# Routed pairs of blocks before the last batch's routing, and two shared tiles at the end (transformer layer with a mixture of experts, one core)

## The reference

```python
x = x + attn(layernorm(x), Wq, Wk, Wv)            # (8, 512, 256), one head
y = layernorm(x)
shared = (silu(y @ sg.T) * (y @ su.T)) @ sd.T     # inner width 512
probs = sigmoid(y @ router.T + bias)
scores, idx = top_k(probs, 2); scores /= scores.sum(-1)
w[t, idx] += scores
routed = einsum(silu(y @ gate_w[e]) * (y @ up_w[e]), down_w[e], w)
x = x + shared + routed
```

## Time and profile before

| | us |
|---|---|
| median of 3 runs | 563.93 |
| lowest and highest run | 558.07, 567.77 |
| span of the profiled execution | 555.3 |
| PE busy in it | 518.0 (93%) |
| DVE, ACT, POOL busy | 369.8, 301.0, 288.9 |
| mean granted PE clock | 0.986 of full |

### The profile page before, as it was taken

One profiled execution on the slowest core, in us unless ns is written; L12 is line 12 of the kernel. 1 busy time (PEld: TensorE's weight loads), 2 busy tenths in 40 slices (PEclk: granted clock), 3 DMA queues, 4 the chain that ended last, 5 costly groups with the idle time before them and its releaser, 6 DMA issues.

```text
span 555.3 us, 14903 instructions
## 1 busy us (share of the span) xinstructions
PE 518.0 (93%) x4757; PEld 425.5 (77%) x4757; DVE 369.8 (67%) x980; ACT 301.0 (54%) x580; POOL 288.9 (52%) x242
## 2 busy tenths in 40 slices
PE   4889988999999999997999999999999999999992
PEld 3557766788878888886767788888787888888881
DVE  5788998689887878899747555445454454454551
ACT  3989877678777676744233443433343433434341
POOL 4466677668676765857022344452444434434443
PEclk9999999899999999998899999999999999999998
DMA  8799848949694947414465965764846536345443
GB/s 271 201 181 208 178 127 158 217 133 209 161 208 141 194 127 170 155 70 136 131 115 85 98 107 69 103 83 60 108 59 89 73 60 97 55 65 78 62 58 38
DMA packets 139351, 68.55 MB, mean 123 GB/s; under 512 B 114608, under 2 KB 132336, under 8 KB 139280
## 3 DMA queue, kind: packets, MB, share of 16 engines
q1 hardware_dynamic: 126128, 48.84, 43.5%
q0 software_dynamic: 13152, 18.76, 19.4%
HBM read 19.46 MB, written 23.08 MB: 77 GB/s over the span
## 4 chain that ended last, share of the span: by engine, by line
PE 65%; DVE 12%; DMA 8%; SPq 5%; ACT 5%; issue 3%; POOL 1%; POOLq 0%; ACTq 0%; DVEq 0%
PE bank L2216 29%; PE bank L2240 15%; PE bank L2547 4%; PE bank L2322 3%; PE bank L2564 3%; DMA v<-xnrow 2%; PE bank L2625 2%; PE bank L2347 2%; PE bank L2392 2%; DMA xn2t<-xrow 2%; PE bank L2369 2%; PE bank L2640 2%; SPq L405 2%; DMA x<-x 1%; DVE h L1470 1%
## 5 line engine op out<-in xcount | busy, mean ns | idle before, releaser
L2216 PE MATMUL bank<-xn2t,w 128*128 128x256 f16 x1608 | 184.9, 273 | 1.3 <-DVE th L1653 1.1
L2216 PEld LDWEIGHTS bank<-xn2t,w 128*128 (+1 forms) x1608 | 155.2, 98 | 24.3 <-DVE th L1653 2.2
L1644 DVE SCALAR_TENSOR_TENSOR th<-th,bank 128x512 f32<-128x512 f32 x83 | 56.6, 682 | 55.2 <-ACT th L989 54.1
L2240 PE MATMUL bank<-w,h 128*128 (+1 forms) x768 | 91.5, 273 | 0.0
L943 ACT ACTIVATE h<-th 128x512 f16<-128x512 f32 (+1 forms) x69 | 42.9, 622 | 84.6 <-DVE th L1653 78.3
L989 ACT ACTIVATE th<-bank 128x512 f32<-128x512 f32 x83 | 49.2, 593 | 62.1 <-PE bank L2216 47.6
L2240 PEld LDWEIGHTS bank<-w,h 128*128 128x128 f16 x768 | 74.0, 98 | 10.4 <-DVE x L1676 0.3
L866 POOL DMA_INDIRECT out<-p,wm x28 | 43.9, 1569 | 67.2 <-ACT p L1323 27.3
L1470 DVE TENSOR_TENSOR h<-th,h 128x512 f16<-128x512 f32 (+1 forms) x69 | 50.6, 733 | 38.3 <-ACT h L943 38.1
L734 POOL TENSOR_TENSOR w<-wst,w 128x768 f16<-128x768 f32 x36 | 59.1, 1645 | 18.9 <-ACT w L943 18.7
L758 POOL DMA_INDIRECT rows<-xrow,sidx x56 | 56.5, 1009 | 17.0 <-issue 13.3
(11 more groups left out here) (188 smaller groups left out, 808.4 us busy)
## 6 DMA issues: line engine op xcount, KB each, us to landing
wst<-w_all SPq DMA_DIRECT2D x36, 384.0 KB
x<-x SPq DMA_DIRECT2D x8, 512.0 KB, 5.6
out<-x SPq DMA_DIRECT2D x8, 512.0 KB, 4.0
rows<-xrow POOLq DMA_DIRECT2D x1, 1192.5 KB, 6.6
rows<-xrow,sidx POOLq DMA_INDIRECT x56
out<-p,wm POOLq DMA_INDIRECT x28
xn2t<-rows SPq DMA_TRANSPOSE x26
wm<-rows SPq DMA_DIRECT2D x26, 9.0 KB, 2.4
```

The costliest lines, as they stand in the source:

```text
L1644: d.scalar_tensor_tensor(out=tb, in0=tb, scalar=1.0, in1=G[half][:, :], op0=ALU.add, op1=ALU.mult).then_inc(f_sg, 1)
L2216: ins = mm(dst, w_ap(j, ws, m * MAT + k * I + (2 * half + i) * P, P), moving(ms * KD + k), start=(cnt == 0), stop=(cnt == 3 * KD - 1))
L2240: ins = mm(o[:, a * D:(a + 1) * D], hb[:, (hs * KI + i) * TT + a * P:(hs * KI + i) * TT + (a + 1) * P], w_ap(j, ws, 2 * MAT + i * D, D), s ...
```

## The change

1. The size of the table of 512-row blocks is set by what six batches surely fill: `QUADS` is 5 instead of 9. Their table is made from the counts after batch 5 (`counts_seen`), while batch 7's attention ends. Blocks are now laid from the beginning of each expert's rows, and the zeros stand behind the last row; they are copied there when the final counts are known (`zero_ends`), so the zeros at the start are one block of 128 rows.
2. PE starts the routed phase after shared tile 12, with three groups that are pairs only (`plain_groups`, pairs 0 to 5). Shared tile 13's down, batch 7's transposes, logits and final counts, and on DVE its routing and the other three tables (pairs, singles, halves, in one chain of 56 steps) are threaded into these groups.
3. Pairs 6 to 25 follow with singles and halves as before, in groups up to 12 (before: up to 11 and a last group with finer pieces). The fifth 512-row block, pairs 24 and 25, is the last. Pairs 8 to 23 are single pairs.
4. `out_base` of batch 7 writes `x1` with attention only. Shared tiles 14 and 15 come at the very end, their inputs being still in SBUF. When all adds have landed, SP reads their rows back from `out` to `x1`, DVE adds the two downs there, and SP writes them with plain DMAs.
5. The weights' last pieces are scaled earlier on ACT, directly one after the other, and made on POOL between the scatters of batch 6.

```diff
-QUADS = (TOPK * T // HP - 7 * E) // 8
+SEEN = 6
+QUADS = -(-(SEEN * S * TOPK - E * (2 * TT - 1)) // (2 * TT))
+EARLY = 2 * (QUADS - 1)
+LATE = 2
+AHEAD = SHARED - LATE
+PLAIN = 3
@@ SP
+            load_pair_rows(pair0, 0, 2 * AHEAD - 2)
+            load_pair_rows(pair1, 1, 2 * AHEAD)
+            load_pair_aux(pair0, 0, 0, 0)
+            load_pair_aux(pair1, 1, 0, 0)
+            out_base(5)
+            out_base(7)
+            out_base(6)
+            for n in (2, 3, 4):
+                pair_rows(n)
+                pair_aux(n)
+            pair_rows(5)
+            zero_ends(0, E // 2)
+            pair_rows(6)
+            zero_ends(E // 2, E)
+            pair_aux(5)
             sp.wait_ge(tab2, T2_STEPS)
+            rows_complete()
...
             sp.wait_ge(y_out, ALL_ADDS)
+            for i in range(LATE):
+                sp.dma_start(tile_of(AHEAD + i), tile_rows(AHEAD + i)).then_inc(back_in[i], 16)
+            sp.wait_ge(y_read, AHEAD + PAIRS + 1)
+            sp.dma_start(tile_rows(AHEAD), tile_of(AHEAD)).then_inc(out_done, 16)
@@ POOL
             w_low(30)
             scatter(5, 5, 8)
             last_identity()
+            w_low(31)
+            w_low(32)
+            scatter(6, 0, 1)
+            w_low(33)
+            scatter(6, 1, 2)
+            w_low(34)
+            scatter(6, 2, 3)
+            w_low(35)
+            scatter(6, 3, 5)
             rstd2(7)
             put_idx(7)
+            scatter(6, 5, 8)
...
+            y_add(0)
+            scatter(7, 0, 4)
+            y_add(1)
+            scatter(7, 4, 8)
+            for n in range(2, 2 * PLAIN):
+                y_add(n)
@@ ACT
             split_h(11, 1)
+            w_scale(32)
+            w_high(32)
             tanh(12, 0)
+            w_scale(33)
+            w_high(33)
             tanh(12, 1)
             split_h(12, 0)
+            w_scale(34)
+            w_high(34)
+            tanh(13, 0)
+            split_h(12, 1)
+            w_scale(35)
+            w_high(35)
@@ DVE
             places(6)
+            ffn_gate(12, 0)
+            ffn_up(12, 0)
+            ffn_gate(12, 1)
+            ffn_up(12, 1)
+            add_shared(10)
+            row_numbers(6)
+            table_of_quads()
+            ffn_low(12, 0)
+            ffn_gate(13, 0)
+            ffn_low(12, 1)
+            add_shared(11)
...
+            def plain_groups():
...
+                ffn_low(t + 1, 1)
+                route(7)
+                ffn(t + 2, 0)
+                weights(7)
+                places(7)
+                row_numbers(7)
+                ffn(t + 2, 1)
+                ffn(t + 3, 0)
+                k = table_of_pairs()
+                ffn(t + 3, 1)
+                k = table_of_singles(k)
+                ffn(t + 4, 0)
+                table_of_halves(k)
+                ffn(t + 4, 1)
@@ PE
             shared_gate_up(13, 0)
-            last_transposes(0)
-            last_transposes(1)
+            shared_down(11, 0, 2)
             shared_gate_up(13, 1)
+            shared_down(12, 0, 2)
...
+            def plain_groups():
+                pair_gate_up(0, 0)
+                shared_down(13, 0, 2)
+                expert(1)
+                pair_gate_up(0, 1)
+                last_transposes(0)
+                last_transposes(1)
+                pair_gate_up(1, 0)
+                expert(2)
+                pair_down(0)
+                pair_gate_up(1, 1)
+                logits(7)
+                pair_gate_up(2, 0)
...
+            def last_group():
+                t = AHEAD + PAIRS
+                gate_up(t, 0, 0, half_batch(xn24(B - 1), 0), True)
+                pair_down(PAIRS - 1)
+                gate_up(t, 1, 0, half_batch(xn24(B - 1), 0), True)
+                gate_up(t + 1, 0, 0, half_batch(xn24(B - 1), 1), True)
+                gate_up(t + 1, 1, 0, half_batch(xn24(B - 1), 1), True)
+                down(t, 0)
+                last_down()
```

More of the change, by code:

```diff
@@ new lines, in zero_ends, with rows_complete @@
+            def zero_ends(first, last):
+                sp.wait_ge(tab2, 2)
+                for e in range(first, last):
+                    end = sp.value_load(end_tab[0:1, e:e + 1], min_val=0, max_val=ROWS - P)
+                    sp.dma_start(rows[ds(end, P), :], rows[SPARE:SPARE + P, :]).then_inc(pads_in, 16)
+            def rows_complete():
+                sp.wait_ge(rows_in[0], scattered(B - 2))
+                sp.wait_ge(rows_in[1], scattered(B - 1))
+                sp.wait_ge(pads_in, 16 * E)
@@ L650, in _ @@
+            for a in range(2):
+                n = 2 * (SHARED - 1) + a
+                sp.wait_ge(z_put, a + 1)
+                sp.dma_start(out[n * P:(n + 1) * P, :], x1[:, n * D:(n + 1) * D]).then_inc(out_done, 16)
+            sp.wait_ge(out_done, 16 * (B + 3))
         @block.gpsimd
@@ L1454, in _ @@
+                if s - FIRST_HALF < HALVES:
+                    half_h(s - FIRST_HALF)
+                ffn_half_and(t + 1, 1, *[PAIRS + SINGLES + s - FIRST_HALF] * (s - FIRST_HALF < HALVES))
+            def last_group():
+                t = AHEAD + PAIRS
+                ffn_half_and(t, 0, PAIRS - 1)
+                y_copy_of(PAIRS - 1)
+                ffn_half(t, 1)
+                ffn_half(t + 1, 0)
+                ffn_half(t + 1, 1)
+            plain_groups()
             first_groups()
-            for i in range(2, GROUPS - 1):
+            for i in range(PLAIN + 2, GROUPS):
@@ L2174, in _ @@
+            plain_groups()
+            first_groups()
+            with dve.Fori(PLAIN + 2, SINGLES - 4 + PLAIN) as i:
                 group(i)
-            group(SINGLES - 4, single=False)
-            for i in range(SINGLES - 3, GROUPS - 1):
+            group(SINGLES - 4 + PLAIN, single=False)
+            for i in range(SINGLES - 3 + PLAIN, GROUPS):
                 group(i, single=False, half=False)
-            ffn(SHARED + PAIRS - 2, 0)
-            ffn(SHARED + PAIRS - 2, 1)
-            ffn(SHARED + PAIRS - 1, 0)
@@ L2679, in group, with last_down @@
                 gate_up(t + 1, 1, expert(2 * i + 1), pair_moving(1), False, covered=True, mats=(1,))
-            def down_parts(t, j, pieces):
-                pe.wait_ge(y_read, t)
-                for low, chunks, parts in pieces:
-                    pe.wait_ge(f_lo, t * 2 + low)
-                    for a in parts:
-                        for i in chunks:
+            def last_down():
+                t = AHEAD + PAIRS + 1
+                pe.wait_ge(fs_h, SINGLES)
+                pe.wait_ge(fh_h, HALVES)
+                pe.wait_ge(ys_read, SINGLES)
+                pe.wait_ge(yh_read, HALVES)
+                for half in range(2):
+                    pe.wait_ge(f_lo, t * 2 + half + 1)
+                    for a in range(2):
+                        for i in (2 * half, 2 * half + 1):
```

761 lines of the change are left out of this document (351 added, 410 removed).

## The result

| | before | after |
|---|---|---|
| median, us | 561.97 (14 runs) | 568.14 (14 runs) |
| lowest and highest | 558.07, 567.77 | 564.78, 576.47 |
| span of the profiled execution | 555.3 | 567.5 |

The ratio is 1.0125, 95% interval 1.0092 to 1.0157: the change makes the kernel slower by some 6 us. The forecast was 561.0, a little faster; the time lies in its range, on the other side of no change.

The account below looks back on a forecast made before the run. TensorE, busy 93% of the span, was taken as the bound. Added 4.0 + 4.2 + 7.5 = 15.7 us against 18.6 removed: 2.9 us less, moving the 563.93 us median to 561.0, range 552 to 571.

Parts of the forecast that it names:

- What is removed: Waits around the old transition 5.3, slow clock 2.5, last tile's wait 0.5, old tail 10.3: together 18.6 us gained.
- One, the approach to pair 0: From shared tile 12 to pair 0, TensorE waits add 4.0 us; bounds 1.0 and 5.6, 2.5 more if the clock falls.
- The holds: Before pair 0, VectorE and GpSimd hold each other during five low parts of weights: 0.5 us added.
- The clock: TensorE's 1.2 GHz level after idling before pair 0: 2.5 us more, only on top of the upper bound.
- term two: Batch 7's routing and tables under three plain groups: TensorE waits add 4.2 us, bounds 1 and 6.
- two or three of 1 to 3 us: Sign of the forecast: that many TensorE waits on low parts of h between 275 and 300 us.
- Three, the end: Tail after TensorE's last matmul, with adds landing, read-back and last additions: 7.5 us, bounds 6.3 and 10.
- Rival D: Chain of adds becomes the bound, falls 5 us behind TensorE, and the readback follows: 566 us; chance 0.12.
- Rival C: Idle TensorE and its slow clock move instead of going, through piece 33's load and VectorE's holds: 570.4 us; chance 0.12.
- pair 0 near 242: Sign of the forecast: pair 0, the first routed work after the shared tiles, starts near 242 us.
- no clock below 1.00: Sign of the forecast: TensorE's clock stays at full level between 240 and 300 us.
- a wait above 3 us before pair 0: Sign that the forecast is wrong: TensorE shows such a wait on the approach to pair 0.

Follow-up runs that it names:

- e_nohold: Changed kernel with GpSimd writing zeros by memset instead of the low parts of weight pieces 31 to 35: ratio 0.9958 to the kernel before.
- e_low_order: Changed kernel with only GpSimd's queue reordered, low part of piece 33 ahead of batch 6's first scatter, 34 and 35 later: ratio 1.0030 to the kernel before.
- e_places: Changed kernel with VectorE making the places of batch 6 ahead of the low part of tile 11's second half: ratio 1.0027 to the kernel before.
- after_timed_b: The changed kernel unedited, timed as a control on the fifth chip: ratio 1.0058 to the kernel before.
- after_again: The changed kernel unedited, run once for a second profile: 560.45 us.
- after_timed: The changed kernel unedited, timed as a control on the second chip: ratio 1.0081 to the kernel before.
- e_front: Changed kernel with VectorE's, GpSimd's and ScalarE's queues reordered before pair 0, batch 7's tables left as they were: ratio 0.9936 to the kernel before.

## Why the prediction was wrong

**What is removed** was right. The second profile of before has it too: 3.1 us of wait on the add, the slow clock behind it, and 10.1 us from the last matmul to the end, all of which the changed kernel no longer has in that form.

**One, the approach to pair 0, is the step that failed**: "I add 0.5: 3.5 + 0.5 = 4.0 us". It measured 10.0 us here, 9.5 to 10.5 in three more profiles of the same kernel, beyond the upper bound of 5.6, and with the clock's 2.5 beyond 8.1. Its walk was sound in one part: tanh of tile 12's second half came 9.4 us after tile 12's start (236.11 and 226.70), for 8.8. Three things in it were not:
- *The holds.* 0.5 us were set for them, in spite of five low parts and rows that showed 4.12 and 1.49. They fell on the table, 2.27 + 2.36, where the walk took 3.0 for it and it took 7.2, and on the low part and the cast around `places(6)`, 1.4 and 1.3: 7.0 us in all beyond the usual lengths. `e_nohold` puts all of them, with the clock that follows the waits, at 6.2 us of distance (21.3 against 27.5, some 0.4 of it perhaps from GpSimd's shorter work), `e_low_order` those in the table at 2.1. The rule of the Trainium skill (SBUF — State Buffer, "SBUF: two separate sides"), which the prediction kept out of its sum, would have given a loss; by that rule and by these rows the held operation ends with the GpSimd instruction (0.02 and 0.04 us behind it).
- *A queue that was not walked.* PE's second half of tile 12 needs `pos` from `places(6)`, which stood behind a low part of tile 11 on VectorE: 2.1 us. Of these 1.4 are the hold of that low part (2.05 us for 0.69), and without it 0.8 is left (`e_nohold`). Taken alone the order costs nothing (`e_places`), since the next wait is longer.
- *The clock.* After both waits TensorE ran at 1.2 GHz for most of a piece, 1.7 + 1.4 = 3.1 us. The text had 2.5 for that, outside the sum, for a wait over 3 us. One of 2.13 us was enough here, and one of 2.00 in `after_timed_b`; in `after_again` and `after_timed` the clock stayed up behind 2.14 and 2.13, and fell behind the longer wait alone.

With the order put right and all else as changed (`e_front`) the kernel is 3.6 us faster than before. The forecast's span was 2.9 us under that of before, so the rest of the sum was about right as a whole, with errors that offset: the distance then loses 2.7 us for 4.0, the tail is 5.3 for 7.5, and the waits of term two are above their 4.2.

**Two, batch 7's preparation**, 4.2 forecast: 1.0 + 3.5 = 4.5 us of waits in the second profile, two of them on low parts, 2.2 the longest, for "two or three of 1 to 3 us". The size holds, one place does not: the 1.0 on the counts is a matmul in PE's own queue ahead of pair 3, which the walk left out. To this come waits of single blocks for transposes, 0.6 to 2.3 us in the three later profiles, that the sum did not have.

**Three, the end**, 7.5 forecast with 6.3 and 10 as bounds: 6.3 here, 5.4 to 7.3 in the four profiles of the kernel, 4.1 to 11.7 over the edits. The mechanism is the forecast's, a lag of the adds that the read-back prolongs; the lower bound was too high, and the spread is wider than both. Rival D had its reason right (the last groups, formerly of pairs only, carry singles and halves) and its place: the chain without halves' adds shows 4.7 us. On the whole it does not set the rate: PE and the chain go at nearly the same 22 to 24 us a group, and the lag is not made good. In `e_nohold`, where PE came earlier, it did set the end.

Added up as the forecast does it, the measured terms are 10.0 + 4.5 + 6.3 = 20.8 us against 18.6 removed: 2.2 us slower, some 3 with the transposes. That is the low end of the 3 to 7 measured. What the first chip's kernel lost beyond it stays open, but for the 4.6 us of idle time and slow clock near 295 in its one profile.

Rival C named the mechanism (piece 33's load and VectorE's holds, idle time and clock); its conditions, 5.6 + 2.5 before pair 0, measured 6.6 + 3.1. It got 0.12 and was the case, at the sign if not at every chip's size. That its 570.4 us lie so near to 568.14 is partly luck: its terms add up to 25.1 us where 20.8 were measured, 8.5 us for batch 7's preparation with its clock where 4.5 came. Of the signs named beforehand, pair 0 near 242 was missed by 12 us (5 of them lie ahead of tile 12's start), "no clock below 1.00" too, and "a wait above 3 us before pair 0" was the sign of error that came. The forecast's 561.0 itself lies under the 561.97 of before, but by 1 us only: three runs had put that kernel at 563.93.

## What to carry to other kernels

When work is moved into the fullest stretch of an engine, list the operations of VectorE there that read two operands from SBUF or cast, and that will meet a GpSimd subtraction, and price each at the whole length of it; then look for the GpSimd instruction that is only there because something ahead of it in its queue waits. Walk each engine's queue to every semaphore of the stretch, TensorE's small products too, before summing waits: one wait taken away is worth nothing while a longer one follows. And if a chain of dependent transfers runs at the pace of the bound engine, its lag is paid in full at the point where something reads its result.

## What was not expected of the hardware

An operation of VectorE can begin before GpSimd's subtraction and still end only with it. At 239.84 one began 0.60 us ahead of the subtraction (240.44), during a scatter with the subtraction queued behind it, and ended 0.02 us after it. Whether the scatter already held it is not shown: times on GpSimd are rough in the profile, and an operation that began with the next such scatter (242.26) took 0.19 us. Scatters without a subtraction behind them held nothing (the table of 2.8 us in `e_low_order` had two beside it). Three subtractions of 256 columns hold VectorE about as long as one of 768, 6.4 us for the table against 7.2, and one operation was held over two of them. And one program with the same queues had tails between 5.4 and 7.3 us and distances between 26.5 and 27.5 in four profiles, with a spread of 8 to 12 us in its times on one chip.
